# Wider rows for the values, the null product first in a half and on 64 rows, and once-only work placed by slot tables

## The reference, cut to what matters

```
q = (layernorm(xn) * g + b) @ Wq           # 16 heads of 64
k, v = split(xn @ Wkv)                     # 16 heads of 64 each
k, v = concat([null_k, k]), concat([null_v, v])    # two learned "null" keys and values per head
q, k = l2norm(q) * q_scale, l2norm(k) * k_scale
sim = 8 * q @ k.T - slope[head] * |distance|       # causal
out = softmax(sim) @ v                     # per head
x + out @ Wout + ffn(xn)                   # ffn(xn) = layernorm(xn) * ln_g + ln_b here
```

## Time and profile before

| | |
|---|---|
| median of 3 runs | 2801.87 us (2801.78 to 2803.41) |
| the profiled execution | 2801.74 us |
| its span, first to last instruction | 2799.7 us |
| PE busy | 2662.4 us, 95% |
| DVE busy | 2516.7 us, 90% |
| ACT busy | 2131.4 us, 76% |
| POOL busy | 2144.4 us, 77% |
| mean granted TensorE clock | 0.985 |

### The profile page before, as it was taken

One profiled execution on the slowest core, in us unless ns is written; L12 is line 12 of the kernel. 1 busy time (PEld: TensorE's weight loads), 2 busy tenths in 40 slices (PEclk: granted clock), 3 DMA queues, 4 the chain that ended last, 5 costly groups with the idle time before them and its releaser, 6 DMA issues. The chain is left out here.

```text
span 2799.7 us, 85007 instructions
## 1 busy us (share of the span) xinstructions
PE 2662.4 (95%) x31631; PEld 1578.3 (56%) x31631; DVE 2516.7 (90%) x6766; ACT 2131.4 (76%) x3381; POOL 2144.4 (77%) x2438
## 2 busy tenths in 40 slices
PE   3689999999999999999999999999999999999997
PEld 2346555556555555555655555555555555555554
DVE  6889999999999999999999999999999999998895
ACT  3577788778777778777887778877887777877775
POOL 5497788977788687987879778897778867797662
PEclk8899999999999999999999999999999999999999
DMA  5223354333542334433444335433344333442222
GB/s 160 56 47 59 67 100 92 86 60 70 101 102 61 67 76 91 104 61 70 84 93 89 65 66 101 88 86 60 73 98 104 59 69 77 85 101 51 53 51 61
DMA packets 629576, 220.19 MB, mean 79 GB/s; under 512 B 593584, under 2 KB 595632, under 8 KB 629168
## 3 DMA queue, kind: packets, MB, share of 16 engines
q1 hardware_dynamic: 627696, 214.67, 37.3%
q10 hardware_dynamic: 1472, 0.09, 0.0%
HBM read 55.23 MB, written 16.78 MB: 26 GB/s over the span
## 5 line engine op out<-in xcount | busy, mean ns | idle before, releaser
L995 DVE CUSTOM_DVE_ANT_0 PS<-PS,STR 128x512 f32<-128x512 f32 (+3 forms) x1536 | 822.1, 580 | 96.4 <-PE PS L1235 92.0
L559 ACT ACTIVATE AR<-PS,SC 128x1024 f32<-128x1024 f32 (+1 forms) x640 | 655.0, 1023 | 130.2 <-PE PS L1246 64.6
L1189 PE MATMUL PS<-WH,XT 128*128 128x388 f16 x2048 | 679.2, 332 | 30.9 <-DVE AR L1008 21.4
L1191 PE MATMUL PS<-WH,XT 128*128 128x388 f16 x2048 | 678.6, 331 | 0.0
L1190 PE MATMUL PS<-WL,XT 128*128 128x388 f16 x2048 | 678.5, 331 | 0.0
L563 ACT ACTIVATE AR<-AR 128x1024 f16<-128x1024 f32 (+1 forms) x640 | 621.7, 971 | 20.3
L765 POOL TENSOR_TENSOR RN<-SS,HALF 128x8 f32<-128x8 f32 x256 | 453.9, 1773 | 193.6 <-DVE SS L1080 191.0
L1036 DVE TENSOR_TENSOR AR<-AR 128x768 f16<-128x768 f32 (+1 forms) x448 | 523.5, 1178 | 9.5 <-ACT AR L563 8.9
L1212 PE MATMUL PS<-AR 64*128 64x512 f16 (+3 forms) x4608 | 497.2, 324 | 6.2 <-ACT AR L559 6.2
L1264 PE MATMUL PS<-AR 128*128 128x66 f16 x4608 | 477.2, 193 | 8.0 <-issue 4.5
L1266 PE MATMUL PS<-AR 128*128 128x64 f16 x4608 | 474.5, 194 | 0.0
(11 more groups left out here) (223 smaller groups left out, 5181.5 us busy)
## 6 DMA issues: line engine op xcount, KB each, us to landing
XW<-in_L_attn_x SPq DMA_DIRECT2D x112, 256.0 KB, 2.9
out<-ACC SPq DMA_DIRECT2D x64, 256.0 KB, 2.2
ACC<-in_L_attn_x SPq DMA_DIRECT2D x56, 256.0 KB, 2.8
AR<-QKB SPq DMA_TRANSPOSE x512, 2.5
AR<-in_L_attn_Wkv SPq DMA_DIRECT2D x2, 1536.0 KB, 13.9
ACC<-in_L_attn_x SPq DMA_DIRECT2D x2, 1024.0 KB, 7.2
AR<-in_L_attn_Wout SPq DMA_DIRECT2D x1, 2048.0 KB, 8.3
AR<-CTK SPq DMA_TRANSPOSE x128, 2.4
```

Of the source, the lines that this page charges most:

```text
L559: e.activation(PR[:, n % 2, :, 0:wide], SB[:, :, 0:wide], ACT.Exp, scale=SIG).then_inc(s_p, 1)
L995: e.tensor_tensor_reduce(out=r[:, 0:n], in0=r[:, 0:n], in1=ST[:, u % 2, h, o:o + n], scale=1.0, scalar=LOW, op0=ALU.add, op1=ALU.max, accu ...
L1189: e.matmul(PJ, XT[:, k, xs], WH[:, k, p, :], start=k == 0, stop=False)
L1191: ins = e.matmul(PJ, XT[:, 4 + k, xs], WH[:, k, p, :], start=False, stop=k == KC - 1)
```

## The change

1. A row of V gets 136 numbers in place of 132, and the low part starts at element 72 in place of 66: the two operands start at byte 0 and 144 of a row of 272 bytes, before at byte 0 and 132 of a row of 264 bytes. V grows, the tiles behind it in the arena AR move up, AR grows from 12,880 to 15,008 numbers, and two weight pieces (WV0, WQ2) get space of their own there. The DMA scratch shrinks from 4096 to 2048.
2. The null product is issued before the value product of its half, from a table of its own (`W_NVP`), and each head's matmul takes 64 rows of PNT and VNT in place of 128. It now starts the accumulation in AV; the last value matmul of each query tile ends it. The transpose's wait and DVE's wait follow (s_nv2, s_av in place of s_o).
3. The `if s == ...` lines of the once-only work become slot tables, some with offsets far below zero; the slots start at -500 in place of -4. The ones and zeros of V are written at the front, before the layer norm, and the masks of VNF (before L862, at the front) move to the DVE step of the null values.
4. All other slot tables have new numbers.

The diff, cut; of the tables two lines stand for all.

```diff
-W_VALUE = [105, 109, 109, 114, 121, 132, 134, 140, 143, 143]
+W_VALUE = [106, 107, 108, 114, 126, 130, 132, 142, 142, 148]
+W_NVP = [105, 112]
...
-LATE_ACT = [0, 1, 5, 6, 9, 10, 15, 16, 18, 24, 25, 27, 32, 33, 38, 39]
-SLOTS = range(-4, SL * NU + 200)
+W_LATA = [-205, -146, -139, -109, -90, -77, -75, -58, -33, -24, 4, 6, 9, 23, 53, 56]
+SLOTS = range(-500, SL * NU + 200)
...
-        AR = sb("AR", [P, 12880], F32)
+        AR = sb("AR", [P, 15008], F32)
-        V = AR[:, 4096:6736].bitcast(F16).rearrange("p (t j c) -> p t j c", t=NV20, j=2)
+        V = AR[:, 4096:6816].bitcast(F16).rearrange("p (t j c) -> p t j c", t=NV20, j=2)
...
                 for u, qc in due(s, W_NTT):
                     w.wait_ge(s_nl, 2 * u + qc + 1)
                     if u:
-                        w.wait_ge(s_o, 2 * (2 * (u - 1) + qc) + 2)
+                        w.wait_ge(s_nv2, 2 * (u - 1) + qc + 1)
...
-                if s in LATE_ACT:
-                    i = LATE_ACT.index(s)
+                for _, i in due(s, W_LATA, 1, BL):
                     src, scale, hi, lo = late(i)
                     e.activation(hi, src, ACT.Copy, scale=scale).then_inc(s_wact, 1)
...
-            w.wait_ge(s_vz, 1)
-            for q in range(4):
-                dc(e.tensor_scalar(VNF[:, :, q, 64], VNF[:, :, q, 64], MSK[:, 8 + q:9 + q], None, ALU.add))
+            dc(e.memset(V[:, :, :, 65:66], 0.0))
+            dc(e.memset(V[:, :, :, 64:65], 1.0))
...
-                        out=V[:, i % NV20, :, 66:130], in0=PJ[:, 260:388].rearrange("p (j c) -> p j c", j=2),
+                        out=V[:, i % NV20, :, 72:136], in0=PJ[:, 260:388].rearrange("p (j c) -> p j c", j=2),
...
                 for u, qc in due(s, W_ON):
                     i = 2 * u + qc
-                    w.wait_ge(s_o, 2 * i + 2)
+                    w.wait_ge(s_av, NS * u + (NS if qc else 3))
...
+                for u, qc in due(s, W_NVP):
+                    w.wait_ge(s_nt[qc], 16 * (u + 1))
+                    w.wait_ge(s_vn, 1)
+                    w.wait_ge(s_on, 2 * u + qc)
+                    for h in range(2):
+                        hs = slice(64 * h, 64 * h + 64)
+                        ins = e.matmul(AV[:, h, :], PNT[hs, qc, h, :], VNT[hs, u % NP, :], start=True, stop=False,
+                                       skip_group_check=True)
+                    ins.then_inc(s_nv2, 1)
...
                     if blocks[0][0] == 0:
-                        w.wait_ge(s_on, 2 * u + qc)
+                        w.wait_ge(s_nv2, 2 * u + qc + 1)
...
-                                e.matmul(AV[:, h, 66 * q:66 * q + 64], PH[:, n % 3, h, pq], VV[:, 66:130], start=False, stop=False,
+                                e.matmul(AV[:, h, 66 * q:66 * q + 64], PH[:, n % 3, h, pq], VV[:, 72:136], start=False, stop=False,
                                          skip_group_check=True)
                                 ins = e.matmul(AV[:, h, 66 * q:66 * q + 66], PL[:, n % 3, h, pq], VV[:, 0:66], start=False,
-                                               stop=False, skip_group_check=True)
+                                               stop=kt == 4 * qc + q, skip_group_check=True)
                     ins.then_inc(s_av, 1)
-                    if blocks[-1][0] == 4 * qc + 3:
-                        w.wait_ge(s_nt[qc], 16 * (u + 1))
-                        w.wait_ge(s_vn, 1)
-                        for h in range(2):
-                            e.matmul(AV[:, h, :], PNT[:, qc, h, :], VNT[:, u % NP, :], start=False, stop=True,
-                                     skip_group_check=True).then_inc(s_o, 1)
```

More of the change, by code:

```diff
@@ new lines @@
+W_OP = [122, 126, 140, 149, 158, 158, 171, 173]
+W_ADD = [115, 119, 139, 151, 158, 158, 163, 165]
+W_PROJ = [z for z in [4, 10, 15, 22, 31, 34, 43, 47] for k in range(KC)]
+W_KV = [3, 10, 18, 25, 33, 34, 44, 47]
+W_VL = [7, 10, 15, 20, 26, 35, 43, 49]
+W_STRIP = [27, 30]
+W_SQ = [14, 28, 46, 48]
+W_SS = [13, 22, 45, 52]
+W_POW = [23, 27, 47, 54]
+W_TP = [39, 49, 61, 70]
+W_HI = [33, 37, 52, 67]
+W_LO = [27, 39, 57, 67]
+W_ROWS = [67, 92]
+W_SHIFT = [69, 95]
+W_CTP = [78, 98]
+W_NX = [77, 95]
+W_NL = [72, 98]
@@ new lines @@
+W_NTT = [85, 101]
+W_XA = [-282, -279, -230, -191, -139, -116, -105, -89]
+W_STAT = [-256, -198, -190, -127, -124, -109, -95, -85]
+W_XB = [-64, -60, -32, -25, -6, -5, 12, 20]
+W_XF = [-55, -43, -32, -9, 1, 6, 13, 15]
+W_XH = [-45, -28, -16, -8, 8, 15, 17, 20]
+W_XL = [-40, -23, -23, -11, 3, 14, 17, 29]
+W_XTP = [-27, -15, -1, 4, 13, 22, 22, 41]
+W_SMALL = [-87, -83, -83, -83, -76]
+W_VSC = [-19]
+W_BASE = [74, 90, 94, 106, 112, 116, 138, 186]
+W_BN = [81, 88, 97, 111, 117, 135, 157, 183]
+W_BM = [76, 84, 97, 110, 119, 133, 153, 180]
@@ L577, in _ @@
                     ln_hi(b, t)
-                if s == 36:
+                for _, i in due(s, W_ALA, 1, BL):
                     w.wait_ge(s_ald, 1)
@@ L1219, in _ @@
                                 ins.then_inc(s_st, 1)
-                if s == 47:
-                    w.wait_ge(s_wo, 1)
-                    e.transpose(PS[0:1, 2, 0:P], AM[:, 5:6], IDF[:, :]).then_inc(s_won, 1)
-                if s == 51:
-                    w.wait_ge(s_wop, 1)
-                    e.matmul(PS[:, 2, P:P + 1], ONE[0:1, :], M8[0:1, :], start=True, stop=True).then_inc(s_won, 1)
+                for _, i in due(s, W_WOT, 1, BL):
+                    if i == 0:
+                        w.wait_ge(s_wo, 1)
+                        e.transpose(PS[0:1, 2, 0:P], AM[:, 5:6], IDF[:, :]).then_inc(s_won, 1)
+                    else:
+                        w.wait_ge(s_wop, 1)
+                        e.matmul(PS[:, 2, P:P + 1], ONE[0:1, :], M8[0:1, :], start=True, stop=True).then_inc(s_won, 1)
                 for u, i in due(s, W_PIECE):
```

170 lines of the change are left out of this document (72 added, 98 removed).

## The result

The changed kernel takes 2848.77 us (median of 4 runs, 2847.8 to 2851.69) against 2801.82 us before (2797.94 to 2803.41): ratio 1.0165, 95% interval 1.0153 to 1.0178. It is 47 us slower, where 2778 us was forecast. Beside the slot tables one more number set changed, `HOLD`: three holding times by which `ring_order` hands out the PSUM banks, 6.4, 6.7 and 6.8 slots before and 9.2, 9.6 and 10.7 now.

A forecast was written before the change was run, and what follows sets the result against it. PE was taken to bound common units, DVE and POOL those behind batch starts. Of 33.5 us less PE stream 26.4 would be realised; with +3 at the start and -0.3 at the end, 2801.74 becomes 2778 us, range 2755 to 2797.

The forecast's parts named there:

- The tables: New slot numbers throughout: seams stay, counted as 0; bounds 16 us either way, a third of the seams' 50 us.
- My own sign of being wrong: One listed sign: common unit above 40.5 us with PE gaps at the scores (exponential late) or pieces (DVE late).
- DVE, with 38.18 us, has room in a unit of 40.2.: Common units: PE sets the pace, so its saved stream, 0.52 us per unit, counts at full price in 40 units.
- DVE becomes the bound everywhere: Rival: DVE's busy time and small gaps already need 40.5 us, only 0.2 us per common unit won; 2797 us, chance 0.07.
- The wider rows: Third value matmul: an operand start off 8 bytes costs 4.3 ns, 4608 times; saves 19.8 us of PE, bounds 0 and 23.
- The null product: Pair on 64 rows per head runs side by side: saves 14.1 us of PE, less 0.4 for row changes; bounds 8 to 14.
- The realised share: Part of PE's 33.5 us saving that shortens the time: full in 40 units, half in 21, none in three; 26.4 us.
- The start: Once-only work moved to the front, partly given back between later evictions: +3 us, bounds -4 and +9.
- the first eviction: Unit 0's first eviction on ACT, at 74.26 before, comes some 6 us later behind added weight blocks and a copy.
- The chain to the null numbers at L582: ACT waits 0.3 us for DVE's shift chain, absorbed by 1.03 us idle: 0, bounds 0 and 64 x 0.3 us.
- the slower rival: ACT stands at L582 for DVE's late chain, delaying a score exponential and PE's scores; 2811 us, chance 0.07.

The follow-up runs named there:

- the run with columns 68 to 131: The kernel before with only the low part of the values moved to columns 68 to 131 (from 66) of the same 132-column row: 0.9981, 2799.14 us.

## Why the prediction was wrong

- **The tables, taken as 0 with bounds of 16 us.** This is the step that failed. Their new order, with POOL's work where it then falls, costs 66 us of waits on PE. I had looked for their effect in the seams alone. Of units 4 to 59, 28 are common, and they went from 40.76 to 41.37 us (17 us); the other 28, in seven seams of four, went from 169.5 to 173.6 us per four (28 us). The order was there to read: the last low part now stands ahead of the maximum of piece 0, whose bank PE asks for 0.9 us after that piece (1295.16 less 0.78 of idle, against 1293.44). What could not be read from the order is that POOL's L783 would begin 0.05 us ahead of that low part and stretch it. My own sign of being wrong, a common unit above 40.5 us with PE's gaps at the pieces, is what came.
- **"DVE, with 38.18 us, has room in a unit of 40.2."** A sum of busy time over a unit says nothing on a queue at one place. DVE's 38.49 and 37.18 us are below the 42.70 and 39.70 of those units too, and PE waits for it in both. The rival "DVE becomes the bound everywhere" had the engine right, but its price, no gain at all, is far from a loss.
- **The wider rows, 19.8 us.** The cause, the start address, was right; that it takes 16 bytes and not 8 the two heads of the run with columns 68 to 131 show (8 past a multiple costs 33.3 ns). The size was off: 17 us at L1279 and 11 back at L1277, 5.7 us in this kernel. I had priced one distance of a chain of three and left the others fixed.
- **The null product, 14.1 us less 0.4.** Right: 15.4 us of stream with it and the order's row changes, 12 us of time by itself.
- **The realised share, 26.4 of 33.5.** Too high: of both edits' 20.5 us on the old slots half came through.
- **The start, +3, and the first eviction "some 6 us later".** The eviction came as said: ACT's L534 is at 80.98, against 74.26. The term was within its bounds but too large: unit 3 starts at 191.9 us, before at 191.6. From there on the once-only work is over. All the loss lies behind it.
- **The chain to the null numbers at L582, 0.** Right: PE's idle time ahead of the scores for ACT's exponential is 6.6 us, before 6.2; the slower rival that I priced never acted. The slower outcome came by a mechanism that I had not listed.

The start of ACT's loop in the changed kernel, to answer:

```profile
71.25 5.89 ACT L592 ACTIVATE WH<-AR,OT 128x768 f16<-128x768 f32 x7 [0.56 <-DVE MX L987]
78.94 2.14 ACT L592 ACTIVATE WH<-AR,OT 128x768 f16<-128x768 f32 x3
80.98 0.25 ACT L534 ACTIVATE QKB<-PS 128x128 f32<-128x128 f32 x1
```

Sum: -5.7 - 15.4 + 65.9 = +44.8 us, and 1 to 2 us at the two ends. What stays open: which of the new slots beside the last low part's make the other half of the waits, what the new `HOLD` does, and why the first distance of a value triple grows in the wide rows.

## What to carry to other kernels

When a hand-made order changes, an engine's busy share over a unit proves no room. Look up, for every bank or tile that the bound engine asks for again soon, what now stands ahead of the instruction that frees it, and which engine works beside that one. Look too at which of the two begins first: 0.05 us decided here who was slowed. A slot can't be restored alone: each has a distance to keep on both sides, and six changes of that kind to the changed kernel gave nothing or cost up to 10% (3123 against 2849 us). If two small edits are to be had, make them on the old order: the null pair on 64 rows in place (2790.87 us), with or without the low values at column 68 (2792.47 us), beats both kernels.

## What the runs showed of the hardware

- A moving operand of 128 bytes per row that starts on 16 bytes lets the next matmul start after 28.4 ns, and 8 bytes past one after 33.3 (the two heads of the run with columns 68 to 131). Part of it comes back at the matmul before: 31.0 instead of 29.5 ns there, in the wide rows 29 or 36 ns. In the wide rows one in eight still needs 33 ns or more.
- Two matmuls of 64 rows and 264 columns on the two halves of the array start 3 ns apart, where two of 128 rows need 112. A change between 64 and 128 rows costs about 0.1 us (12.8 us for 126 more of them).
- After 3.1 us without work PE's granted clock stood at 0.50, and 512 columns took 0.42 us each for the next 5 us.
- DVE's subtraction of 768 elements per row in SBUF takes 0.95 us alone, beside a memset of POOL or beside POOL's operations on 8 elements. It took 1.80 to 1.84 us in all 38 cases in which POOL's multiplication of 512 elements had begun 0.02 to 0.06 us before it. In 25 cases DVE began first, with 1024 elements: it kept its 1.22 us, and POOL took 2.0 to 2.1 us in place of 1.04.
